# Merge, norm and routing of the first layer woven into the attention loop of a two-layer kernel

## What is computed

```
x = x + L0_attention(layernorm(x), ctx, ctx)   # 16 heads of 8 dimensions, rotary, softmax, out-projection Wm
x = x + L0_ffn(layernorm(x))                   # 64 experts, top 8, weights of softmax(logits)
x = x + L1_attention(layernorm(x), ctx, ctx)   # attention over features
x = x + L1_ffn(layernorm(x))                   # 16 experts, top 4

# in L0_attention, for each batch b and head h (n = m = 256 positions):
prob = softmax(q[b,:,h,:].T @ k[b,:,h,:] / sqrt(8));  heads = prob @ v;  out = Wm @ heads + bm
# in L0_ffn: logits = x @ gate_w.T; the 8 largest of 64 choose the experts; combine by softmax weight
```

## Time and profile before

| what | us |
|---|---|
| median of 3 runs | 812.78 (810.65 to 813.86) |
| the profiled execution: its own time | 811.38 |
| its span (first to last instruction) | 809.3 |
| attention: first scored head to last copy of sums | 82.7 to 198.0 |
| first scatter to end of last scatter | 231.9 to 313.1 |
| first load of held_phase | 319.6 |
| busy in the span: PE, DVE, ACT, POOL | 483.3, 365.7, 204.3, 339.5 |

### The profile page before, as it was taken

One profiled execution on the slowest core, in us unless ns is written; L12 is line 12 of the kernel. 1 busy time (PEld: TensorE's weight loads), 2 busy tenths in 40 slices (PEclk: granted clock), 3 DMA queues, 4 the chain that ended last, 5 costly groups with the idle time before them and its releaser, 6 DMA issues. The chain is left out here.

```text
span 809.3 us, 11268 instructions
## 1 busy us (share of the span) xinstructions
PE 483.3 (60%) x3381; PEld 374.5 (46%) x3381; DVE 365.7 (45%) x1201; ACT 204.3 (25%) x525; POOL 339.5 (42%) x464
## 2 busy tenths in 40 slices
PE   2717998996655000898799940533520598988930
PEld 1602544552643000787678830323420587878820
DVE  8946766760467100344344423588760122222216
ACT  0530765775111000332223310120200222222200
POOL 8564212220047774265355460003153366666610
PEclk9965999998685555899999985555655699999975
DMA  4294488875993333799985226700007198999816
GB/s 157 71 209 111 134 228 259 278 259 177 389 353 154 153 156 113 244 309 316 328 281 191 93 95 213 320 0 20 0 21 204 48 303 277 284 291 287 255 38 254
DMA packets 78736, 159.30 MB, mean 197 GB/s; under 512 B 12267, under 2 KB 47093, under 8 KB 76896
## 3 DMA queue, kind: packets, MB, share of 16 engines
q1 hardware_dynamic: 55776, 109.72, 42.5%
q0 software_dynamic: 13168, 32.02, 11.5%
q10 hardware_dynamic: 9744, 16.98, 6.0%
HBM read 105.05 MB, written 56.12 MB: 199 GB/s over the span
## 5 line engine op out<-in xcount | busy, mean ns | idle before, releaser
L558 DVE TENSOR_REDUCE at_top<-at_ps_top 128x2 f32<-128x512 f32 x128 | 82.7, 687 | 47.0 <-PE at_ps_top L498 46.1
L1031 POOL DMA_INDIRECT held<-e_extended,e_address x64 | 62.0, 968 | 69.5 <-DVE e_address L1023 50.3
L1507 POOL DMA_INDIRECT rows<-hd_out,hd_rows x64 | 62.2, 972 | 67.5 <-DVE hd_out L1458 44.5
L1360 PE MATMUL hd_ps_up<-hd_x_turned,e_w 128*128 128x160 f32 x512 | 84.4, 309 | 0.0
L591 ACT ACTIVATE at_prob<-at_ps_score 128x512 f32<-128x512 f32 x128 | 72.3, 595 | 44.9 <-PE at_ps_score L516 44.8
L1665 PE MATMUL l_ps_up<-l_x_turned,e_up_w 128*112 128x128 f32 x672 | 82.4, 277 | 0.0
L1665 PEld LDWEIGHTS l_ps_up<-l_x_turned,e_up_w 128*112 128x112 f32 x672 | 81.2, 181 | 2.6
L1360 PEld LDWEIGHTS hd_ps_up<-hd_x_turned,e_w 128*128 128x128 f32 x512 | 77.8, 196 | 8.8 <-issue 6.2
L1495 DVE TENSOR_TENSOR hd_inner<-hd_silu,hd_ps_up 128x160 f32<-128x160 f32 x64 | 20.6, 321 | 119.7 <-ACT hd_silu L1445 119.7
L853 POOL DMA_INDIRECT table<-choice,ft_r_address x32 | 30.6, 957 | 103.9 <-DVE ft_r_address L844 95.1
L498 PE MATMUL at_ps_top<-op_k_in,op_q_in 96*128 96x256 bf16 x256 | 54.4, 300 | 23.1 <-PEq L110 21.0
(11 more groups left out here) (280 smaller groups left out, 902.1 us busy)
## 6 DMA issues: line engine op xcount, KB each, us to landing
e_w<-in_weights SPq DMA_DIRECT2D x64, 384.0 KB, 11.9
e_up_w<-in_up SPq DMA_DIRECT2D x42, 448.0 KB, 4.1
held<-at_empty ACTq DMA_DIRECT2D x16, 960.0 KB, 5.7
hd_rows<-held SPq DMA_DIRECT2D x15, 768.0 KB, 12.7
e_down_w<-in_down SPq DMA_DIRECT2D x42, 224.0 KB, 4.9
ft_g_rows<-rows SPq DMA_DIRECT2D x8, 1024.0 KB, 13.4
parts<-op_parts SPq DMA_DIRECT2D x8, 576.0 KB, 7.1
attended<-at_out SPq DMA_DIRECT2D x8, 512.0 KB, 6.9
```

What stands on the lines that cost most here:

```text
L558: nc.vector.reduce_max(top[:, 2 * h:2 * h + 2], ps_top[at % TOPS][:], AX_X).then_inc(top_found, 1)
L1031: self.nc.gpsimd.indirect_dma_start(self.held_dram, to, self.held.extended[:, b, :], None)\
L1360: op = nc.tensor.matmul(ps_up[e % 2][:, part, :], w[:, k, part * P:(part + 1) * P], x_turned[g % 2][:, j, k, :], start=k == 0, stop=k == 1)
L1507: nc.gpsimd.indirect_dma_start(rows_out, to, out_ap, None, bounds_check=TOKENS * LAYER0.chosen - 1, oob_is_err=False).then_inc(semaphore, 16)
```

## The change

`merge_phase` is gone. Its work stands in `attend_phase`, in the same loops over `at`, one batch at a time and at fixed offsets: the sums of batch b are loaded at step 16b + 22, divided at 16b + 34, multiplied by Wm at + 35, added and measured at + 36, normalised at + 37, turned at + 39, scored at + 41, ranked at + 43 and scattered at + 46 to + 49 and + 54 to + 57. The loops run 36 steps past the last head, POOL's 56.

What goes with it: the sums come back from HBM with heads as rows (`by_head`, `load_packed`), numerators and sums side by side as two 128x256 tiles, so that both sets of transposes and the copy L1181 fall away, and the reciprocal is over 128x256 instead of two times 128x16. The value bias goes through Wm once (`lift`). The root takes two instructions for each Newton step instead of three (`Rstd`), the scaling itself moves from DVE to ACT (`act_normalise`), as do the expert weights (`act_weights`). `ps_out` has one buffer instead of two, which pays for a bank that merging and routing share. The fill is issued every 4 steps from step -20. The operand loads of batches 4 to 7 and the 32 weight loads move to ACT's queue; the weights go into the SBUF of operands that are done (`arena`), one load every second step from step 85 on.

```diff
+class Rstd:
...
+        for _ in range(NEWTON):
+            link(nc.vector.scalar_tensor_tensor(work, root, half, root, ALU.mult, ALU.mult))
+            link(nc.vector.scalar_tensor_tensor(root, work, 1.5, root, ALU.add, ALU.mult))
+        nc.vector.scalar_tensor_tensor(shift, self.mean_var[:, 0:1], -1.0, root, ALU.mult, ALU.mult).then_inc(ready, 1)
...
+    def pool_scatter(self, pool, b, k):
+
+        if k == 0:
+            pool.wait_ge(self.places_ready, b + 1)
+            pool.wait_ge(self.weights_ready, b + 1)
+        to = bass.IndirectOffsetOnAxis(ap=self.held.address[:, b, k:k + 1], axis=0)
+        self.nc.gpsimd.indirect_dma_start(self.held_dram, to, self.held.extended[:, b, :], None).then_inc(self.held.scattered, 16)
...
+    LOAD_AT, SHARE_AT, MERGE_AT, ADD_AT, TURN_AT, SCORE_AT, RANK_AT, SCATTER_AT = 22, 34, 35, 36, 39, 41, 43, 46
+    END = B * H + 36
...
+        def batch_at(at, offset):
+
+            b, late = divmod(at - offset, H)
+            return b if late == 0 and 0 <= b < B else None
...
+            def load_packed(b):
+                if b >= 2:
+                    sp.wait_ge(divided, b - 1)
+                for p in (2 * b, 2 * b + 1):
+                    sp.wait_ge(stored[p % 4], 16 * (p // 4 + 1))
+                by_head = attended[b].rearrange("g (j v) n -> (g j) v n", v=VW)
+                for k in range(2):
+                    sp.dma_start(packed[b % 2][:, k, :], by_head[:, k * HD:(k + 1) * HD, :]).then_inc(packed_loaded[b % 2], 16)
...
+            for at in range(-LEAD, END + LEAD):
+                if at == SCATTER_AT:
+                    held.pool_wait_emptied(pool)
+                hh, late = divmod(at + LEAD, HALF)
+                if late == HALF - 1 and hh < HALVES:
+                    cut_tops(hh)
+                for k in range(LAYER0.chosen):
+                    b = batch_at(at, SCATTER_AT + k % 4 + k // 4 * HALF)
+                    if b is not None:
+                        routing.pool_scatter(pool, b, k)
...
+            def divide(b):
+                dve.wait_ge(packed_loaded[b % 2], 32 * (b // 2 + 1))
+                link(nc.vector.reciprocal(share[:], packed[b % 2][:, 1, :]))
+                if b >= 1:
+                    dve.wait_ge(merged, b)
+                nc.vector.tensor_tensor(heads[:], packed[b % 2][:, 0, :], share[:], ALU.mult).then_inc(divided, 1)
...
+            for at in range(-LEAD, END):
+                if at + LEAD < B * H:
+                    find_top(at + LEAD)
...
+                b = batch_at(at, SHARE_AT)
+                if b is not None:
+                    divide(b)
+                b = batch_at(at, ADD_AT)
+                if b is not None:
+                    add(b)
...
+            waiting = list(range(ring.SLOTS))
+            for at in range(-LEAD, END):
+                if at % 4 == 0 and 0 <= (at + LEAD) // 4 < GROUPS:
+                    held.act_empty(act, (at + LEAD) // 4)
+                b = batch_at(at, H + 4)
+                if b is not None and b + DEEP < B:
+                    act.wait_ge(weighted, 4 * (b + 1))
+                    operands.load(act, b + DEEP)
...
+                if at >= (DEEP + 1) * H + 4 and at % 2 == 1 and waiting:
+                    e = waiting[0]
+                    if ring.free_after[e] * H + 4 < at:
+                        act.wait_ge(weighted, 4 * ring.free_after[e])
+                        ring.load(act, waiting.pop(0))
```

More of the change, by code:

```diff
@@ L351, in cut_low @@
                                         ALU.subtract).then_inc(low_cut, 1)
+            nc.gpsimd.memset(held.empty[:], SKIP_FLOAT).then_inc(held.empty_set, 1)
             for b in range(B):
@@ new lines, in act_exponentials, with pe_rank @@
+    def act_exponentials(self, act, b):
+        act.wait_ge(self.top_known, b + 1)
+        self.nc.scalar.activation(self.expo[:], self.logits[:], ACT.Exp, bias=self.minus_top[:],
+                                  accum_out=self.total[:]).then_inc(self.expo_ready, 1)
+    def pe_rank(self, pe, b):
+        nc, to = self.nc, self.ps_rank
+        pe.wait_ge(self.logits_read, b + 1)
+        nc.tensor.matmul(to, self.consts.ones[:], self.consts.bases[:, 0:self.layer.experts], start=True, stop=False)
+        for before in range(b):
+            nc.tensor.matmul(to, self.consts.ones[:], self.held.mask[:, before, :], start=False, stop=False)
+        pe.wait_ge(self.mask_ready, b + 1)
+        nc.tensor.matmul(to, self.consts.earlier[:], self.held.mask[:, b, :], start=False, stop=True).then_inc(self.ranked, 1)
@@ new lines, in dve_targets @@
+    def dve_targets(self, dve, link, b):
+        targets = self.held.extended.bitcast(I32)[:, b, D + 1::2]
+        dve.wait_ge(self.mask_ready, b + 1)
+        link.free(self.nc.vector.tensor_tensor_scan(targets, self.consts.ones[:, 0:self.layer.experts], self.held.mask[:, b, :],
+                                                    self.consts.more[:, SLOTS_AT + b:SLOTS_AT + b + 1], ALU.mult, ALU.add))
+        dve.wait_ge(self.expo_ready, b + 1)
+        self.nc.vector.reciprocal(self.share[:], self.total[:]).then_inc(self.share_ready, 1)
```

771 lines of the change are left out of this document (346 added, 425 removed).

## The result

| | before | changed |
|---|---|---|
| median, us | 812.57 (810.65 to 813.86, 4 runs) | 780.28 (776.06 to 783.77, 4 runs) |
| ratio, 95% interval | 1 | 0.9602 (0.9551 to 0.9654) |
| the profiled execution, us | 811.38 | 776.06 |

The forecast was 770 with a range of 745 to 800. The time went down by 32 us where 42 were forecast. The changed kernel was run once more beside the first experiments: 780.34 (774.04 to 785.29, 6 runs), ratio 0.9610 (0.9556 to 0.9664).

The account below looks back on a forecast made before the run. It took the serial 122.2 us from attention's end to held_phase's first load, and DVE's pace in the attention loop, as the bounds; attention +41 and the stretch behind it -83 gave -42, so 770 us, range 745 to 800.

Parts of the forecast that it names:

- The tail, -83 us: From attention's end to held_phase's first load: 39.6 us where it was 122.2, so -83 us.
- my 23.0 us: Batch 7's chain behind attention, from copy of sums through store, load and division to places, before its 8 scatters: 23.0 us.
- Bursts, +43 us: Steps 34 to 43 of each 16-step period: DVE's added work and waits cost 8.6 us in batches 0 to 4, +43 us.
- The rival "crowding": PE's waits for the division lower TensorE's clock, hand-overs lengthen: +3 us a burst, +15, 785 us; chance 0.09.
- Row copies, -8 us: Attention loop: row-copy waits behind operand loads in SP's queue go with those loads on ACT's queue and a slower loop, -8 us.
- ACT, 0 us: Steps 0 to 33: ACT's work of 28.9 us fits the 30.7 us they took; weight loads also cost nothing: 0 us.
- that rival (up to 900 us): ACT's queue is held by its own DMAs, 21 weight loads between exponentials: up to 900 us; chance 0.06.
- The last 24 steps, +3 us,: Steps 108 to 131, without maxima: batch 5 is worked there, ACT and PE wait for DVE's norm, +3 us.
- Crowding, +3 us,: Everything closer together for DMA and clock, fills within the first 60 us: +3 us, a guess between 0 and 15.
- A plain reciprocal (751): Rival "faster": reciprocal is a plain pass, 1.7 us less in six batches, and hand-overs hide: 751 us; chance 0.17.
- The exposed chain (798): Each in-order queue waits for the next; heads stand for a batch's chain, burst 20.3 instead of 16.5: 798 us; chance 0.15.
- The late fill (818): POOL waits at step 46 for all 17 fills; landing at attention's end, they leave 64 scatters behind it: 818 us; chance 0.03.

Follow-up runs that it names:

- the second profile: Profile of the changed kernel run again without an edit: 780.34 us (6 runs), ratio 0.9610 to the kernel before; the profiled execution took 780.8 us.
- the second reciprocal: Changed kernel with the 128x256 reciprocal done twice in each batch: 787.29 us (6 runs), 7.0 us more than the changed kernel.
- wider links: Changed kernel with Wm, sum, turning, logits and ranks at later steps (+36, +37, +41, +43, +45): 779.64 us (6 runs), ratio 0.9583 to the kernel before.
- the three edits together: Changed kernel with sums loaded behind row copies, copy of sums ahead of operand loads, weight loads paused from step 128 to 142: 765.78 us (5 runs), ratio 0.9433.

## Why the prediction was right, and 10 us too low

**What bounds the kernel** and **what the change removes** were read rightly: a serial stretch of 121.7 us became one of 44.9 and 42.6, the scatters of batches 0 to 6 left the path, and their spacing of 1.27 us stayed.

**The tail, -83 us, came out as -77 and -79.** The step that failed is "store 4.5 and load 5.2 (half the size of the store of 6.9)". Load and reciprocal of batch 7 in the changed kernel:

```profile
249.72 1.17 SPq L995 DMA_DIRECT2D at_packed<-attended  x2
...
255.50 1.75 DVE L1144 RECIPROCAL at_share<-at_packed 128x256 f32<-128x256 f32 x1 [3.12 <-DMA at_packed<-attended]
```

From the end of the last copy, 239.91, to the load it is 9.8 us, then 5.8 to the division, then 12.4 to the first scatter at 267.93; of my 23.0 us what came behind the load was also 12.4 (2.6 + 0.6 + 3.0 + 3.2 + 2.2 + 0.8). In the second profile they are 6.8 and 6.5 us. I had halved the store for its size and left out the weight loads that are under way beside it; with a pause of these loads the first part is 5.0 us, and the kernel 7.2 us faster. The Trainium skill (DMA: Bandwidth & Descriptors, Issuing engines are not separate DMA queues) has the rule, that DMAs of all issuers share the 16 engines, which I had set aside for the row copies: here the trace agrees with it, loads issued by ACT delayed a store issued by SP.

**Bursts, +43 us.** The number was near, its parts weren't. The reciprocal takes 1.74 us instead of 2.1. A batch puts 25 instructions on DVE, not 24; in the period from 147.98 to 167.52 they take about 7.4 us with the gaps between them, where I had 7.8. From the cut of step 35 to that of 107 my terms (65.4 - 8 + 43, less some 2.5 for the first division, which lies ahead) give 98 us; it was 92.6 and 96.3. That DVE's added work counts in full where it stands is shown by the second reciprocal. DVE's waits came out smaller where TensorE's clock held. Two of the burst's 8 heads and 8 heads between, columns as in the earlier trace rows, the granted clock third from the end:

```profile
167.50:178.40 10.90, 10.01 (x83) 5.06 (x82) 9.07 (x30) 6.16 (x16) 5.57 (x12) 0.84 0.69 176
178.40:186.90 8.50, 6.52 (x62) 3.20 (x63) 7.48 (x12) 5.13 (x11) 5.54 (x12) 1.00 0.40 144
...
207.80:220.60 12.80, 10.69 (x75) 5.61 (x74) 9.04 (x29) 6.06 (x14) 5.52 (x12) 0.70 0.69 235
```

DVE does the same 9.0 us in both bursts; at a clock of 0.70 the 8 heads take 1.9 us more than at 0.84. The rival "crowding", with its +3 us a burst, thus has part of the truth, and the spread of the executions goes with it; that the clock is the cause was not shown by a run, and wider links did not change it.

**Row copies, -8 us.** This step failed as I put it. The waits of before are gone, but their place is taken by one of 6.84 us. I had seen that "The load of the sums waits in SP's queue for a store to land (6.9 us), ahead of a row copy" and charged nothing, since "in the slow stretches a half batch takes 9 us". That holds for every batch but the first, whose load comes at step 22, ahead of the first burst at 34: there the loop has its old pace of 0.8 us a step. With the load behind the row copies the kernel is 6.0 us faster. And the credit given to ACT's queue isn't due: back on SP the loads cost no net time, and from the second batch on no row copy is late from either queue, but for 0.75 us at the end. What is left is the slower pace, which I had named second, or the fill, which now ends at 134.8 instead of 182.3 (DMA share from 136 to 160 us with the loads on SP 0.68, before 0.92); no run tells these two apart.

**ACT, 0 us.** ACT stood behind its four operand loads for 9.4 us in four times, 2.83 at the most, and PE for 3.6. I had added up ACT's work for steps 0 to 33, 28.9 of 30.7 us, and not looked at what four issues in a row hold up with a single `ps_out`: up to step 27 attention lost 4.1 us beyond its later start, 2.5 of them here (without the loads on ACT this part took 1.5 us less, against the second profile 3.4). The weight loads, which I feared more, took 0.33 to 0.38 us an issue up to 237; that rival (up to 900 us) looked at the wrong loads.

**The last 24 steps, +3 us,** were +1.0 and +2.0. **Crowding, +3 us,** stands for a start 2.0 and 2.8 us later, whose cause is open.

**The rivals.** A plain reciprocal (751) fell with 1.74 us. The exposed chain (798) was there in part: ACT waited up to 3.5 us in each period for the norm. The kernel with the root on POOL shows that 1.7 us more in that link bring it out nearly in full. The late fill (818) didn't come; the last piece was issued at 134.8 and POOL stood for it nowhere.

Summed up for the profiled execution: +13.8 us up to step 35 (forecast 5.5, the crowding and the first division), +27.2 to step 107 (forecast 32.5), +1.0 behind it (3), -76.8 for the rest (-83): -34.8, and 0.5 of it elsewhere, -35.3 in all against -42. The second profile has +15.3, +31.0, +2.0 and -79.1, with 0.2 elsewhere, -30.6 in all. That the profiled sum came so near is in part luck: up to step 35 it took 8.3 us more than forecast and the tail gave 6 less, and the bursts and the last 24 steps, 5.3 and 2.0 us under their terms, took half of that back.

## What to carry to other kernels

When work is woven into a loop, price it by the pace at the step where it stands, first period apart from the others: a wait that a slow loop hides is paid in full before the loop has become slow. In an in-order queue put what waits for a round trip through HBM behind what the next heads need, and keep bulk loads out of the stretch in which a small store and its load are the path. Work moved to an idle engine pays only if the engines that wait for it in order have something else first; and the same move can be right under the loop and wrong behind it.

## What the hardware showed that was not expected

The reciprocal of 128x256 took 1743 to 1753 ns in all eight cases, 6.8 ns an element, where the product of the same size takes 425. The Trainium skill (VectorE: DVE Perf Modes, First, the fixed hardware budget) says that it is an iterative divide with a repeat count of 8. Read as 8 cycles an element, which that section does not say, and with the 0.96 GHz of that page, an estimate would be 256 x 8 / 0.96 ns = 2.13 us; the trace has less, and decides.

Scatters beside DVE, in order of time, in the middle of attention and beside the plan for full experts:

```profile
164.63 1.74 DVE L1144 RECIPROCAL at_share<-at_packed 128x256 f32<-128x256 f32 x1
...
165.43 0.96 POOL L845 DMA_INDIRECT held<-e_extended,e_address  x1 [0.30 <-issue]
...
270.32 0.62 DVE L905 TENSOR_TENSOR at_p_inside<-more,at_p_count 128x448 f32<-128x448 f32 x1
...
270.46 1.30 POOL L845 DMA_INDIRECT held<-e_extended,e_address  x1 [0.31 <-issue]
```

Beside a reciprocal from SBUF a scatter keeps its 0.96 us and the spacing of 1.26. Beside a DVE instruction with two tiles from SBUF it does not: the scatter that starts during the 128x448 comparison of the plan takes 1.28 to 1.31 us in every profile of a changed kernel, and 1.12 in the kernel before (265.19 us, beside L1091 at 264.87). With the three edits together one takes 1.11 us beside the product L1147. The Trainium skill (SBUF — State Buffer, SBUF: two separate sides) names DVE instructions with two inputs from SBUF among those that take the port pair it shares with GpSimd. That is the rule that spoke against the change, and the trace agrees with it, but in single scatters and for 0.15 to 0.35 us each; of the last eight, for which I had worked out 3.4 us by it, only one is longer. That "the rows show no such wait" was not so, but to charge nothing was right to within 0.4 us.

Small instructions of 128x1 cost 0.19 to 0.35 us on POOL and 0.14 to 0.22 on DVE, so the ten of the root take 3.6 us instead of 1.9 (root on POOL, and changed kernel).
